# Four-layer f32 network: attention in 32-row quadrants, with maxima and softmax sums moved by DMA

## The reference, cut to what matters

```python
# layer 0                                  # layer 3: sets of keys
att = einsum('bqhd,bkhd->bhqk', q, k)      logits = einsum(q * scale, k)
att = att * scale / temperature            l = where(key_mask, logits, -inf)
bias = slopes * (k_pos - q_pos)            a = softmax(l)
att += where(causal, bias, -inf)           out = einsum(a, v)
y = softmax(att) @ v                       reg_out = (x_pos + x_neg) * 0.5   # first 5 tokens
return y @ W_proj + b_proj                 return out @ W_proj + b_proj
```

## Time and profile before

| | us |
|---|---|
| median of 3 runs | 4843.78 |
| the profiled execution, device time | 4840.89 |
| its span in the trace | 4839.0 |
| PE busy | 4549.0 (94%) |
| DVE busy | 2544.5 (53%) |
| ACT busy | 1674.0 (35%) |
| POOL busy | 48.9 (1%) |

### The profile page before, as it was taken

How to read it: one execution, slowest core, us unless ns; L and a number is a source line. 1 busy time by engine, 2 the same in 40 slices (tenths; PEclk the granted TensorE clock), 3 DMA queues, 4 the chain that set the end, 5 groups by cost and what they waited for, 6 DMA issues and landing times. The chain is left out here.

```text
span 4839.0 us, 58787 instructions
## 1 busy us (share of the span) xinstructions
PE 4549.0 (94%) x20997; PEld 2683.9 (55%) x20997; DVE 2544.5 (53%) x5867; ACT 1674.0 (35%) x3173; POOL 48.9 (1%) x36
## 2 busy tenths in 40 slices
PE   7999989999999999999999997999797896899997
PEld 3554546756666676666667665666465443333333
DVE  6666653242523325252332523887777776566764
ACT  3444432232222223223232322444342221355554
POOL 0000000000000000000000000000000000000000
PEclk9999999999999999999999998999998898899999
DMA  2000011111111111111111111000000000000001
GB/s 78 14 17 15 15 61 53 70 53 57 66 53 62 61 63 60 53 54 69 62 61 56 49 70 49 1 0 1 0 1 17 1 1 16 19 14 19 14 18 39
DMA packets 47767, 179.15 MB, mean 37 GB/s; under 512 B 12376, under 2 KB 20704, under 8 KB 30184
## 3 DMA queue, kind: packets, MB, share of 16 engines
q1 hardware_dynamic: 47488, 175.35, 10.5%
HBM read 152.76 MB, written 4.19 MB: 32 GB/s over the span
## 5 line engine op out<-in xcount | busy, mean ns | idle before, releaser
L1013 PE MATMUL l_exp_out<-l_w,l_hidden 128*128 128x256 f32 x4096 | 914.0, 384 | 0.3
L1003 PE MATMUL l_hid<-l_xn_t,l_w 128*128 128x512 f32 x2048 | 895.3, 595 | 15.3 <-ACT l_hidden L1132 15.3
L1013 PEld LDWEIGHTS l_exp_out<-l_w,l_hidden 128*128 128x128 f32 x4096 | 782.9, 193 | 118.6 <-issue 9.2
L1132 ACT ACTIVATE l_hidden<-l_hid,l_w 128x512 f32<-128x512 f32 x512 | 350.8, 687 | 1017.5 <-PE l_hid L1003 1017.5
L1003 PEld LDWEIGHTS l_hid<-l_xn_t,l_w 128*128 128x128 f32 x2048 | 390.2, 191 | 490.8 <-issue 466.4
L428 DVE TENSOR_REDUCE l3f_row_max<-l3f_bank 128x1 f32<-128x512 f32 x512 | 328.5, 685 | 178.2 <-PE l3f_bank L316 177.8
L1270 DVE SCALAR_TENSOR_TENSOR l_moe<-l_exp_out,l_gates,l_moe 128x256 f32<-128x256 f32 x256 | 123.6, 483 | 485.3 <-PE l_exp_out L1013 480.6
L399 ACT ACTIVATE l3f_prob_t<-l3f_bank 128x512 f32<-128x512 f32 x512 | 278.0, 595 | 275.3 <-PE l3f_bank L323 275.1
L323 PE MATMUL l3f_bank<-l3f_q_t,l3f_k_t 32*128 32x512 f32 x1024 | 313.8, 640 | 1.4 <-ACT l3f_prob_t L399 1.3
L425 DVE CUSTOM_DVE_ANT_0 l_masked<-l_bank,l_mask 128x384 f32<-128x384 f32 (+3 forms) x512 | 229.1, 488 | 161.0 <-PE l_bank L316 159.1
L316 PE MATMUL l3f_bank<-l3f_k_t,l3f_q_t 32*128 32x512 f32 x1024 | 301.6, 657 | 8.5 <-DMA l3f_q_t<-l3f_set_rows_q 7.4
(11 more groups left out here) (448 smaller groups left out, 6178.8 us busy)
## 6 DMA issues: line engine op xcount, KB each, us to landing
l_w<-in_w SPq DMA_DIRECT2D x128, 1024.0 KB, 5.0
all_x<-in_x SPq DMA_DIRECT2D x8, 512.0 KB, 11.0
l_q_t<-l_packed SPq DMA_DIRECT2D x128, 32.0 KB
l_k_t<-l_packed SPq DMA_DIRECT2D x128, 32.0 KB
l3f_q_t<-l3f_packed SPq DMA_DIRECT2D x128, 32.0 KB
l3f_k_t<-l3f_packed SPq DMA_DIRECT2D x128, 32.0 KB
out_x<-all_x SPq DMA_DIRECT2D x8, 512.0 KB, 5.7
l_hidden<-in_fp4w SPq DMA_DIRECT2D x1, 2304.0 KB
```

The costliest lines, as they stand in the source:

```text
L1003: ins = nc.tensor.matmul(bank[:, :], w1[:, e % 2, c, f * P:(f + 1) * P], xn_t[:, c, :], start=c == 0, stop=c == CT - 1)
L1013: ins = nc.tensor.matmul(bank[:, 0:C], hidden[:, e % 2, f, j * P:(j + 1) * P], w2[:, e % 2, f, :], start=f == 0, stop=f == HF - 1)
L1132: hid.empty(nc.scalar.activation(hidden[:, e % 2, f, :], bank[:, :], ACT.Relu, bias=w[:, B1][:, e * HF + f:e * HF + f + 1]), (e, f))
```

## The change: what it does

- Order and distance: block B comes directly behind block A, then maxima, then V. `AHEAD` is 7 instead of 5.
- Maxima: they are stored side by side (16 columns), turned by one transpose, copied and negated by ScalarE, and put into q_t's maximum rows by 4 DMAs (`sync`). The subtraction on VectorE goes. `score_t` of a group waits for `max_moved`.
- Sums: the values have 16 columns of ones, so the sum stands on 16 rows, next to y's 16 rows. 8 DMAs per group gather y and sums as [128, 512] halves (`y_packed`, `sums`), and `divide` (two per tile: step 12 for the first half, step 4 of the next tile for the second) takes a reciprocal of [128, 512] and multiplies straight into y_t. The transposes of y and the second ones to y_t go.
- Causal mask: the diagonal matmuls go. 8 rows of q_t and k_t (`halves`, filled by 32 DMAs at the start) add -1e30 where a block's upper half of keys meets its lower half of queries, and GpSimd clears the rest of the 128 x 128 block of prob_t with `affine_select`, two heads at a time; V waits for `selected`.
- SyncE: its loop now follows the steps; each step first calls `sync`, and the moves of groups stand at steps 7, 8, 12 and 0.
- Sets stage: reg_q comes by 4 more DMAs per group instead of VectorE, and the mean over the registers is added to y_t.

```diff
-    AHEAD = TJ + 1
+    AHEAD = TJ + 3
...
-            nc.vector.memset(self.v[:, i, :, :, D:D + 1], 1.0)
-            nc.vector.memset(self.v[:, i, :, :, D + 1:self.VD], 0.0)
+            nc.vector.memset(self.v[:, i, :, :, D:self.VD], 1.0)
...
+    def group_of_maxima(self, t):
+
+        g, i = divmod(t + self.AHEAD, TJ)
+        return g - 1 if i == 0 and 0 <= g - 1 < B * G else None
+
+    def group_of_sums(self, t):
+
+        g, i = divmod(t - TJ - 1, TJ)
+        return g if i == 0 and 0 <= g < B * G else None
+
...
-                flow.wait_emptied(pe, ("t", u, s))
+                if not self.causal:
+                    flow.wait_emptied(pe, ("t", u, s))
+                elif s % 2 == 0:
+                    pe.wait_ge(self.selected, 2 * u + s // 2 + 1)
...
+            flow.fill(nc.tensor.transpose(bank[0:TJ * HPG, 0:P], self.row_max[:, g % 2, :], ident), ("mx", g))
...
-                flow.wait_emptied(pe, ("mx", t // TJ))
+                pe.wait_ge(self.max_moved, 16 * TJ * (t // TJ + 1))
             score_t(0)
             score_t(1)
         if 0 <= w < n:
             score(2)
             score(3)
-        if 0 <= t < n:
-            diagonal(0)
-            diagonal(1)
-        if 0 <= t - 1 < n:
-            values(t - 1)
-        if t % TJ == TJ - 1 and 0 <= t + 1 < n:
-            maxima((t + 1) // TJ)
-        if 0 <= w < n:
             score(0)
             score(1)
         if 0 <= t < n:
             score_t(2)
             score_t(3)
-            diagonal(2)
-            diagonal(3)
-        if t % TJ == 2 and 0 <= t - TJ < n:
-            transposes(t // TJ - 1)
+        if self.group_of_maxima(t) is not None:
+            maxima(self.group_of_maxima(t))
+        if 0 <= t - 1 < n:
+            values(t - 1)
...
+        g = self.group_of_sums(t)
+        if g is not None:
+            if g >= 2:
+                self.wait_y_moved(act, g - 2)
+            bank = flow.wait_filled(act, ("y", g))
+            flow.empty(nc.scalar.activation(self.y_rows[:, g % 2, :], bank[:, :], ACT.Copy), ("y", g))
         if 0 <= t < n:
             u = t - 2
             if u >= 0 and u % TJ < TJ - 1:
                 act.wait_ge(self.pv_done, u // TJ * (TJ - 1) + u % TJ + 1)
-            exponential(0)
-            exponential(1)
-        if t % TJ == 0 and 0 <= t - 1 < n:
-            g = t // TJ - 1
+            for s in range(HPG):
+                exponential(s)
+        g = self.group_of_maxima(t)
+        if g is not None:
             if g >= 2:
-                flow.wait_filled(act, ("yn", g - 2))
-            bank = flow.wait_filled(act, ("y", g))
-            flow.empty(nc.scalar.activation(self.y_rows[:, g % 2, :], bank[:, :], ACT.Copy), ("y", g))
-        if 0 <= t < n:
-            exponential(2)
-            exponential(3)
-
-    def vector(self, nc, dve, t, steps, y, mask):
+                act.wait_ge(self.max_moved, 16 * TJ * (g - 1))
+            bank = flow.wait_filled(act, ("mx", g))
+            flow.empty(nc.scalar.activation(self.max_rows[:, g % 2, :], bank[0:TJ * HPG, 0:P], ACT.Copy, scale=-1.0), ("mx", g))
+
+    def gpsimd(self, nc, pool, t):
+
+        for s in (0, 2):
+            for h in (s, s + 1):
+                self.flow.wait_emptied(pool, ("t", t, h))
+            block = self.prob_t[:, t % 2, s:s + 2, 0:P]
+            nc.gpsimd.affine_select(block, block, [[0, 2], [1, P]], ALU.is_ge, 0.0, 0, -1).then_inc(self.selected, 1)
...
+    def divide(self, nc, dve, steps, b, u, y_t):
+
+        self.wait_y_moved(dve, b * G + 2 * u)
+        self.wait_y_moved(dve, b * G + 2 * u + 1)
+        steps.link(nc.vector.reciprocal(self.sums[:, u, :], self.sums[:, u, :]))
+        nc.vector.tensor_tensor(y_t[:, u, :], self.y_packed[:, u, :], self.sums[:, u, :], ALU.mult).then_inc(self.divided, 1)
+
+    def sync(self, sp, t):
+
+        g = self.group_of_sums(t)
+        if g is not None:
+            b, i = divmod(g, G)
+            u, first = i // 2, i % 2 * HPG
+            self.flow.wait_emptied(sp, ("y", g))
+            if b:
+                sp.wait_ge(self.divided, 2 * (b - 1) + u + 1)
+            for s in range(HPG):
+                for part, to in ((0, self.y_packed), (D, self.sums)):
+                    sp.dma_start(to[(first + s) * D:(first + s + 1) * D, u, :],
+                                 self.y_rows[s * SLOT + part:s * SLOT + part + D, g % 2, :]).then_inc(self.y_moved[i], 16)
+        g = self.group_of_maxima(t)
+        if g is not None:
+            self.flow.wait_emptied(sp, ("mx", g))
+            for qt in range(TJ):
+                sp.dma_start(self.q_t[self.MAX_ROW::SLOT, g % G, qt * P:(qt + 1) * P],
+                             self.max_rows[qt * HPG:(qt + 1) * HPG, g % 2, :]).then_inc(self.max_moved, 16)
...
@@ layer0, SyncE @@
+            sp.wait_ge(halves_ready, 1)
+            for s in range(HPG):
+                rows = slice(s * SLOT + att.MAX_ROW + 1, s * SLOT + att.MAX_ROW + 1 + TJ)
+                for g in range(G):
+                    sp.dma_start(att.q_t[rows, g, :], halves[:, 0, :]).then_inc(halves_moved, 16)
+                    sp.dma_start(att.k_t[rows, g, :], halves[:, 1, :]).then_inc(halves_moved, 16)
...
+            for t in TIMES:
+                b, i = divmod(t, att.STEPS)
+                att.sync(sp, t)
+                if (b, i) == (-1, 7):
                     sp.wait_ge(alibi_loaded, 32 * HPG)
-                for g in range(G):
-                    if b:
-                        att.wait_group_over(sp, b - 1, g)
-                    att.move(sp, b, g)
-                    sp.dma_start(att.q_t[att.MAX_ROW::SLOT, g, :], alibi_dram[0][att.MAX_ROW::SLOT, g, :]).then_inc(att.q_moved[g], 16)
+                    sp.wait_ge(halves_moved, 32 * HPG * G)
+                if i in MOVES:
+                    g = MOVES.index(i)
+                    tile = b + 1 if g < G - 1 else b
+                    if 0 <= tile < B:
+                        if tile:
+                            att.wait_group_over(sp, tile - 1, g)
+                        att.move(sp, tile, g)
+                        sp.dma_start(att.q_t[att.MAX_ROW::SLOT, g, :], alibi_dram[0][att.MAX_ROW::SLOT, g, :]).then_inc(att.q_moved[g], 16)
...
+                if i == 12 and 0 <= b < B:
+                    if b:
+                        flow.wait_filled(dve, ("p", b - 1, 1))
+                    att.divide(nc, dve, st, b, 0, y_t)
+                if i == 4 and b >= 1:
+                    att.divide(nc, dve, st, b - 1, 1, y_t)
...
@@ layer3_sets, SyncE @@
+            for t in TIMES:
+                b, i = divmod(t, att.STEPS)
+                att.sync(sp, t)
+                if i in MOVES:
+                    g = MOVES.index(i)
+                    tile = b + 1 if g < G - 1 else b
+                    if 0 <= tile < B:
+                        flow.wait_emptied(sp, ("setq", tile))
+                        flow.wait_emptied(sp, ("setk", tile))
+                        if tile:
+                            att.wait_group_over(sp, tile - 1, g)
+                            flow.wait_filled(sp, ("rs", tile - 1))
+                        if tile:
+                            sp.wait_ge(reg_ready, tile)
+                        att.move(sp, tile, g)
+                        for s in range(HPG):
+                            head = g % 2 * HPG + s
+                            sp.dma_start(reg_q[s * SLOT:s * SLOT + D, g, :],
+                                         att.packed[head * D:(head + 1) * D, 0, g // 2, 0:REG]).then_inc(att.q_moved[g], 16)
+                            rows = slice(s * SLOT + D, s * SLOT + att.MAX_ROW + 1)
+                            sp.dma_start(att.q_t[rows, g, :], set_rows_q[rows, :]).then_inc(att.q_moved[g], 16)
+                            sp.dma_start(att.k_t[rows, g, :], set_rows_k[rows, :]).then_inc(att.k_moved[g], 16)
```

More of the change, by code:

```diff
@@ L322, in score_t @@
             bank = flow.open(pe, "score_t", ("t", t, s))
-            ins = nc.tensor.matmul(bank[:, 0:T - q.start], self.k_t[rows, g, kb * P:(kb + 1) * P], self.q_t[rows, g, q],
-                                   start=True, stop=not self.causal)
-            if not self.causal:
-                flow.fill(ins, ("t", t, s))
-        def diagonal(s):
-            if self.causal:
-                flow.fill(nc.tensor.matmul(flow.bank(("t", t, s))[:, 0:P], mask_eye, mask_t, start=False, stop=True), ("t", t, s))
+            flow.fill(nc.tensor.matmul(bank[:, 0:T - q.start], self.k_t[rows, g, kb * P:(kb + 1) * P], self.q_t[rows, g, q],
+                                       start=True, stop=True), ("t", t, s))
         def values(u):
@@ L708, in _ @@
                     roots(2, slice(FIRST, B))
+        @block.gpsimd
+        def _(pool):
+            for t in range(att.ALL):
+                att.gpsimd(nc, pool, t)
         @block.vector
@@ L803, in _ @@
             V.memset(xn_t[:, :, 0:1], 0.0)
+            st.link(V.memset(halves, 0.0))
             V.memset(mask[:, 0:T - P], 0.0)
@@ L2719, in last_tile @@
```

(5 more changed lines are left out.)

159 lines of the change are left out of this document (55 added, 104 removed).

## The result

The changed kernel takes **5076.14 us** (median of 4 runs, 5068.06 to 5079.22) against 4844.54 (4 runs): ratio **1.0476**, 95% interval 1.0458 to 1.0494. It is 4.8% slower; the forecast was 5010 us, the range 4870 to 5080.

The account below looks back on a forecast made before the run. TensorE's own order of work was taken to bound the kernel. Sets +123, causal +32 and clock +11 us made 4840.9 + 166 = 5007, and 2.9 for the runs' median gave 5010 us, range 4870 to 5080.

Parts of the forecast that it names:

- likeliest case: Whole kernel: the forecast of 5010 us with its own spread, 4930 to 5075 us, chance 0.60.
- Order: Both stages: head 3's score_t waits for head 0's bank; net +3.5 us a sets tile, -3.3 a causal tile.
- Divide: VectorE, twice a tile: 4.1 us in one piece delays what is queued behind it; 0 to 135 us, 89 taken.
- Step 5 causal: Causal stage: TensorE waits for a bank whose maximum stands behind the divide and dx; +4.1 us, seven tiles, +29.
- Step 4 sets: Sets stage: the registers' maximum and exponential come late behind the divide; +4.4 us, seven tiles, +31.
- Step 12: Work behind the divide comes late: sets stage +2.4 us, eight tiles, +19; causal stage +1.2, eight tiles, +10.
- SyncE: Sets stage: 128 DMAs a tile in one ordered queue make step 12's maxima late; +5.2 us, seven tiles, +36.
- Clock: TensorE runs at a lower clock around stalls: 1.5 us charged to each of the seven longest, +11.
- Starts and ends: Stage starts wait for DMAs, ends for y's gather and divide: sets +6 and +6.6 us, causal +12 and +6.6.
- Only the order costs: Rival: divides and DMAs are absorbed, only head 3's score_t wait stays; about 4872 us (4852 to 4930), chance 0.17.
- GpSimd bounds: Rival: GpSimd's clears, at 3.1 us each, bound the causal stage; 5200 us; GpSimd or worse above 5075, chance 0.07.
- Faster: Rival: banks free in time for head 3's score_t, so TensorE gains its removed work; 4720 us, chance 0.13.

Follow-up runs that it names:

- run with five repairs: Seven-repairs kernel, but values again behind both score blocks and y copied at the next step's start: 4928.96 us, 1.0181 of the kernel before.
- short reciprocal: Changed kernel with the reciprocal taken of 16 of the 512 columns (output not the reference's): 4983.37 us, 1.0303 of the kernel before.
- GpSimd's queue: Changed kernel with the sets stage's transfers of sums and maxima issued by GpSimd instead of SyncE: 5036.77 us, 1.0407 of the kernel before.
- clock-kept run: Changed kernel plus four unused 128x512 matmuls in the causal stage's step 5, ahead of the waiting transpose: 5072.39 us, 1.0480 of the kernel before.
- order put back: Changed kernel with V between block A and block B again, maxima still last: 5042.34 us, 1.0423 of the kernel before.
- order repaired: Here the kernel with all seven repairs, V between the score blocks among them: 4824.06 us, 0.9961 of the kernel before.
- four repairs: Changed kernel with V between blocks, GpSimd issuing the sets stage's sums and maxima, divides in thirds, halves by 8 DMAs; together 4892.88 us, 1.0105 of before.
- three more: Added to the four: y copied between exponentials, GpSimd issuing small DMAs beside moves, second divide clear of step 4; 4824.06 us, 0.9961 of before.

## Why the prediction was right, and what was off in size

The side was right, and every wait that the sum charges is seen in the traces; the sum (+166) was 70 us short of the +236 measured. That the time fell inside the range was close: 5076 is 4 us below its upper end and 1 us above the spread given to the likeliest case. It was also helped by errors of opposite sign. By the terms below, some 31 us were charged too much (the waits at steps 4 and 12) and some 110 too little (clock 54, causal stage 27, starts and ends 18, sets tiles 10); the 9 us by which this overshoots 70 stay unassigned.

The signs named in advance came out so: head 3's score_t starts 1.87 us after the first in the sets stage (forecast 1.8; 2.94 before), a step without a job takes 4.06 us (3.86), tiles are 102.4 and 81.9 us (98 and 78), and SyncE issues for 75% of a sets tile (80%).

- **Order.** Forecast: 8.5 us a sets tile for the order, 5.0 back for what leaves. The run with five repairs measures the order at 8.4 and, against before, +5.0 a tile net (forecast +3.5). In the causal stage the order cost 6.5 of 8.0, but far less came back than the 11.3 counted: with the divide's stall out (short reciprocal) a tile is 75.7, +0.1, where -3.3 was forecast: 27 us over the stage. That is the first mis-sized term. The prediction let all the removed work come back as time, but waits took its place in part: in that run TensorE stands still for 2.5 us a tile (0.2 before), for VectorE's maxima, banks of score_t and copies of q, k and v. Where the rest of these 3.4 us went isn't shown.
- **Divide.** Step 5 causal: 4.05 us, forecast 4.1. Step 4 sets: 2.70, and head 3's score_t comes up to 0.95 us later than in other steps, part of it half clock; forecast 4.4. Step 12: 0.3 (sets) and 0.6 (causal), forecast 2.4 and 1.2. In the sets stage the queue's stall at that place covers it; with GpSimd's queue it appeared, 1.7 a tile. Removed nearly as a whole it gave 93 us, with its clock and 6 us at the two ends, where 89 were forecast without either.
- **SyncE.** The seven stalls of the sets stage are 4.66 to 5.84 us, forecast 5.2. SyncE's issues took 0.59 (packed rows) and 0.65 to 0.68 us (set rows), near the 0.62 and 0.69 of the rows; the two kinds that no row showed took 0.57 (reg_q) and 0.52 (maxima), where 0.62 was taken.
- **Clock.** This term was mis-sized most. I charged 1.5 us to each of seven stalls, from one place at a stage's end where little work follows. In the middle every long stall pays: the clock-kept run shows 2.5 us a causal tile, and in the sets stage 102.4 less the 87.0 of a tile with neither stall (the run with five repairs, so another kernel in other things too) is 15.4, of which 8.5 are waits (5.2, 2.7 and 0.6) and 6.9 the clock, 3.4 a stall. 7 x 2.5 + 14 x 3.4 = 65 us instead of 11. The granted clock itself agrees: the stretches at 0.50 shown above would make 7.8 us a sets tile and 2.7 a causal one. The Trainium skill ("TensorE: Matmul & The Clock Gate", Part 1) says that the array runs throttled until activity releases it; these windows agree (0.50 after the wait, 1.00 later), and it was in the prediction with too few places.
- **Starts and ends.** Sets +8 and +8 for 6 and 6.6. Causal +21 and +12 for 12 and 6.6: the halves took the 20 us of issue that were counted (forecast 22), but the first move was issued at 42.0, the x loads taking 7.3 of SyncE's time at its end. The end: from the start of the last V to the projection 13.1 us, and the 16 matmuls take 6.5 at half clock.
- **GpSimd.** A clear takes 483 ns in the mean (estimate 0.8) and cost nothing: V starts at least 0.47 us behind the clear that it waits for, mostly over 2 (with the order put back, 0.05 in a dozen steps). The lock-out between the two engines, which the prediction cites, shows in the clears. Most take 0.41 us; but 37 of the 256 meet a VectorE instruction with two inputs in SBUF, and each of these ends 0.26 to 0.27 us after that instruction, having taken up to 1.35 us:

```profile
205.71 1.22 DVE L772 SCALAR_TENSOR_TENSOR l_s<-l_s,l_gate 128x1024 f32<-128x1024 f32 x1
205.98 1.22 POOL L419 TENSOR_SCALAR_AFFINE_SELECT l_prob_t<-l_prob_t 128x256 f32<-128x256 f32 x1 [0.48 <-ACT l_prob_t L392]
```

  So it is mostly GpSimd that was late here, where the prediction reckoned with VectorE; the addition to x behind this one takes 1.31 us instead of 1.22. The row maxima of VectorE, with one input in SBUF and one in PSUM, took 686, 553, 420 and 288 ns by size, 688, 555, 421 and 286 before, so they aren't touched.
- **Rivals.** "Only the order costs" falls with the stalls; "GpSimd bounds" with 483 ns. "Faster" gave its condition as banks free in time; with the order repaired it is met, and the tiles are 3.7 and 3.4 us shorter, less than the 11 and 8 that it promised.

## What to carry to other kernels

When a step's transfers, reciprocals and copies are moved off a full engine, price the queue that takes them by its issue count and its order, not by its busy share: 128 issues a tile made SyncE late, and moving a group's later only changed the victim. Charge a stall of the sizes seen here (2.7 to 5.8 us in a dense TensorE stage) with some 3 us more for the clock, and compare the period of a repeated step, since a tile can lose 8 us without one us of idle time in the profile. Where a change moves work well but lands behind its own new stalls, repair order, pieces and queue together: here the four repairs that were run alone gave 4 to 68 us, 145 in all, together 183, and with three more 252.
